# A GRU with routed experts: the order of the first loads, of the bias products and of the first x blocks

## The chip, the cores and the metric

The kernel runs on one core of one Trainium2 chip. The metric is the device time of one execution in microseconds, taken as the median of three runs. TensorE (PE in the profile), VectorE (DVE), ScalarE (ACT), GpSimd (POOL) and SyncE (SP) each run their own instruction stream in order; they meet through semaphores. SP and ACT also issue DMAs, each on a queue of its own (q1 is SP's, q10 is ACT's).

## What is computed

A GRU runs over 256 time steps for a batch of 16 rows of width 512, starting from `cond_2048`. Its states then go through eight low-rank experts, of which each row uses the two that a router picks, and the result is added to x. Cut to what matters:

```python
def cell(h, x):                     # 256 steps, each needs the one before
    gi = x @ W_ih + b_ih            # [16, 512] @ [512, 1536]
    gh = h @ W_hh + b_hh
    r = sigmoid(i_r + h_r)
    z = sigmoid(i_z + h_z)
    n = tanh(i_n + r * h_n)
    return (1 - z) * n + z * h
hs = scan(cell, cond_2048, x)       # x: [16, 256, 512]
logits = hs / norm(hs) @ router_w   # 8 experts, top 2, renormalised
out = x + sum_e combine[:, e] * (hs @ Wa[e] @ Wb[e])
```

## The kernel before

**Tiling.** The width of 512 is K = 4 slices of 128. A block of x is S = 8 time steps of 16 rows, 128 rows in all, and there are 32 blocks. Every fp32 operand is kept as two fp16 parts, a high and a low one, and a product is the sum of three part products (TERMS), so a pair of time steps takes 12 units (4 slices times 3 terms), each of four matmuls that sit side by side in the array and write the four 32-row groups of a PSUM bank. `pair_part(p, units)` does such units of pair p (steps 2p and 2p+1) of x @ W_ih into the bank `pairs[p % 2]`, on top of the biases that already stand there.

**Start.** Before step 0 can run, W_ih and W_hh (four slices each, 768 KB a slice) have to be loaded and split: ACT makes the high part of a third of a slice (`split_weights`, ACT Copy), DVE the low part, in the order of the list SPLITS: 12 entries for W_ih, then 12 for W_hh. The first three blocks of x are not transposed by DMA but by PE (`turn_first(b)`, four fp32 transposes against the identity) and then split by ACT and DVE (`split_first(b)`). The biases are spread over the rows by fp32 matmuls (`put_first_biases`: for each of the two pairs banks one matmul of 512 columns and one of 384), and `keep_biases` copies the sum to SBUF, from where ACT writes it into later banks (`put_biases`). `first_parts(k)` does the three units of slice k of pair 0. `seed(0)` and `seed_z(0)` copy the finished pair 0 from its bank into the banks `gates` and `zbank`, and `first_state_part` adds h @ W_hh: it goes through the four slices with the high weights (each waits for ACT's splits of the slice) and then through the four with the low weights (each waits for DVE's).

**Queues at the start.** ACT issues the four slices of W_ih, with x block 0 between the second and the third. SP issues three bias loads, four pieces of `cond`, the four slices of W_hh, router_w, then x block 1 once slice 1 of W_hh has landed and x block 2 once slice 2 has.

**A step.** In step n PE first does `state_part(n)` (32 matmuls of 256 columns into `gates`, 32 of 128 into `zbank`). DVE transposes the gates (the row `tr<-gates`, once a step), and DVE and ACT work through r, z, n and the new state (`st`), which PE waits for in step n+1. Behind the state part PE does what can be done meanwhile: units of the next pairs (`pair_ahead`), and expert products from step 9 on. The order on PE before step 0 and in it is: pair 0, units 0 to 5 of pair 1, `turn_first(1)`, `first_state_part`, units 6 to 11 of pair 1, `turn_first(2)`. At the end ACT does `split_first(0)` after its ninth split, `keep_biases` after its thirteenth, the seeds after its sixteenth.

Of the kernel before, what the change touches and what calls it, by code (L numbers as in the profile page):

```python
# [12 lines left out]
P = 128  # L13
# [15 lines left out]
def gru_moe_kernel(nc, x, cond, W_ih, W_hh, b_ih, b_hh, router_w, Wa, Wb, out):  # L29
# [23 lines left out]
    with ExitStack() as ctx:  # L53
# [259 lines left out]
        def _(sp):  # L313
# [64 lines left out]
            sp.wait_ge(consts_ready, 2)  # L378
            groups = "(g j c) -> j g c"
            sp.dma_start(bias_h[0:P:32, HN, :], b_hh[2 * D:3 * D].rearrange("(j c) -> j c", j=K)).then_inc(bias_loaded, 16)  # L380
            sp.dma_start(bias_h[0:P:32, RG:ZG + 1, :], b_hh[0:2 * D].rearrange(groups, g=2, j=K)).then_inc(bias_loaded, 16)
            sp.dma_start(bias_i[0:P:32, :, :], b_ih.rearrange(groups, g=3, j=K)).then_inc(bias_loaded, 16)
            for j in range(K):
                sp.dma_start(cond_sb[32 * j:32 * j + B, :], cond[:, j * P:(j + 1) * P]).then_inc(cond_loaded, 16)
            for k in range(K):
                load_hh(k)
            sp.dma_start(rw32[:, :, :], router_w.rearrange("(p k) e -> p k e", k=K)).then_inc(rw_loaded, 16)
            for b in (1, 2):
                sp.wait_ge(whh_loaded[b], 16)
                load_first(b)  # L390
# [14 lines left out]
        def _(pool):  # L405
# [96 lines left out]
            def prepare_state():  # L502
# [4 lines left out]
                pool.wait_ge(primed, 2)  # L507
# [41 lines left out]
        def _(act):  # L549
            for k in range(K):  # L550
                if k == 2:
                    act.dma_start(xin[:, 0, :], x_blocks[0]).then_inc(first_loaded[0], 16)
                act.dma_start(wih32[:, k, :, :].rearrange("p g n -> p (g n)"), W_ih[k * P:(k + 1) * P, :]
                              ).then_inc(wih_loaded[k], 16)
# [107 lines left out]
            def beside(n):  # L662
# [16 lines left out]
                if n == 0:  # L679
                    split_first(2)  # L680
# [14 lines left out]

            act.wait_ge(consts_ready, 4)
            nc.scalar.activation(table_use[:, :], ones[:, :], ACT.Sigmoid)
            for n in range(N_GRU_SPLITS):
                split_weights(n)
                if n == 8:  # L700
                    split_first(0)
                if n == N_IH_SPLITS:
                    keep_biases()
                    copy_high(-1)
                    act.wait_ge(consts_ready, N_CONST)
                if n == N_IH_SPLITS + 3:
                    seed(0)
                    seed_z(0)
            split_first(1)
# [7 lines left out]
        def _(dve):  # L717
# [117 lines left out]
            def beside(n):  # L835
# [7 lines left out]
                if n < FIRST - 1:  # L843
                    split_first(n + 1)
# [10 lines left out]
            for n in range(N_GRU_SPLITS):  # L855
                split_weights(n)
                if n == 8:
# [3 lines left out]
                if n == N_IH_SPLITS:  # L861
# [8 lines left out]
        def _(pe):  # L870
# [29 lines left out]
            def pair_part(p, units):  # L900
# [3 lines left out]
                if 0 in units:  # L904
                    if p == 1:
                        pe.wait_ge(bias_kept, 1)
# [11 lines left out]
            def put_first_biases():  # L918

                pe.wait_ge(bias_loaded, 16 * 3)  # L920
                for bank in pairs:
                    nc.tensor.matmul(bank[:, 0:4 * P], spread_rows[:, :],
                                     bias_h[:, :, :].rearrange("p g c -> p (g c)"), start=True, stop=False,
                                     skip_group_check=True)
                    mm = nc.tensor.matmul(bank[:, P:4 * P], spread_rows[:, :],
                                          bias_i[:, :, :].rearrange("p g c -> p (g c)"), start=False, stop=True,
                                          skip_group_check=True)
                mm.then_inc(bias_done, 1)
# [134 lines left out]
            def pair_ahead(n):  # L1063
# [4 lines left out]
                if p < T // 2:  # L1068
                    pair_part(p, range(UNITS[s]) if n % 2 else range(UNITS[s - 1] if n else 6, UNITS[s] if n else all_units))
# [80 lines left out]
```

## Time and profile before

| | us |
|---|---|
| median of three runs | 1009.57 |
| the three runs | 1009.29, 1009.57, 1010.45 |
| the profiled execution | 1010.27 |
| span of the profiled execution | 1008.5 |
| PE busy | 977.9 (97%) |
| DVE busy | 878.0 (87%) |
| ACT busy | 689.5 (68%) |

The span is what the profile shows, from the first instruction to the last; 1.77 us of the profiled execution lie around it. The shares say little about the change, which touches only the first 35 us or so: there PE waits for loads, and from step 0 on the steps follow one another with nothing between them.

### The profile page before, as it was taken

Reading aid. Unit: us, or ns where it says so; the run is one execution under the profiler, and the core shown is the slowest. Engines: PE = TensorE matmul, PEld = TensorE weight load, DVE = VectorE, ACT = ScalarE, POOL = GpSimd, SP = SyncE. Lnnn points to the kernel's source line nnn. Section 1 sums busy time; section 2 is a strip of 40 time slices with the busy share of each in tenths; the row PEclk is TensorE's granted clock in tenths of the full one; section 3 lists DMA queues with packets and bytes.
Section 4 is the critical chain, followed back from the end, with each engine's and each line's share of the span. In section 5 each row is a group of like instructions: output and inputs, shape, how many; then the busy total and the mean of one; then the engine's idle time right before and its main releaser. Section 6 shows DMA issues by size and latency. Waiting matters only on the chain.

```text
span 1008.5 us, 60534 instructions
## 1 busy us (share of the span) xinstructions
PE 977.9 (97%) x28939; PEld 668.9 (66%) x20799; DVE 878.0 (87%) x3637; ACT 689.5 (68%) x2696; POOL 292.9 (29%) x755
## 2 busy tenths in 40 slices
PE   4789999999999999999999999999999999999997
PEld 2456666666667666677666666666676676676674
DVE  6889888888888888888888888888888888888887
ACT  6687766776766676666677676677666667666664
POOL 1032323332323332323332332332233332233223
PEclk9999999999999999999999999999999999999999
DMA  8321111111111111111111111101111101110000
GB/s 298 93 81 31 28 33 31 27 30 32 29 31 33 28 27 35 27 31 33 29 25 35 28 32 29 33 23 35 30 30 30 32 22 35 31 30 20 14 9 29
DMA packets 49360, 38.83 MB, mean 39 GB/s; under 512 B 34532, under 2 KB 38972, under 8 KB 49084
## 3 DMA queue, kind: packets, MB, share of 16 engines
q1 hardware_dynamic: 48236, 31.41, 11.5%
q8 instruction: 198, 3.24, 1.3%
q10 hardware_dynamic: 848, 3.54, 1.0%
q14 instruction: 78, 0.64, 0.2%
HBM read 18.94 MB, written 8.39 MB: 27 GB/s over the span
## 4 chain that ended last, share of the span: by engine, by line
PE 91%; DVE 4%; DMA 2%; ACT 1%; issue 1%; SPq 0%; POOL 0%; DVEq 0%; POOLq 0%
PE pairs L882 17%; PE ybank L882 12%; PE gates L962 11%; PE gates L967 11%; PE pairs L873 8%; PE ybank L873 5%; PE zbank L882 5%; PE zbank L873 5%; PE obank L882 5%; PE nbank L882 5%; PE obank L873 3%; PE nbank L873 3%; DMA whh<-in_L_cond_W_hh 1%; DVE tr L747 1%; PE ybank L999 1%; DMA xin<-in_x 1%
## 5 line engine op out<-in xcount | busy, mean ns | idle before, releaser
L882 PE MATMUL pairs<-wx,xs 128*32 128x384 f16 x4096 | 281.4, 328 | 0.2 <-DVE wx L727 0.2
L609 ACT ACTIVATE rr<-pre 128x64 f32<-128x64 f32 x256 | 65.7, 257 | 245.8 <-DVE pre L750 245.8
L882 PE MATMUL ybank<-hparts,wa 128*128 128x128 f16 x2048 | 194.1, 219 | 0.0
L882 PEld LDWEIGHTS ybank<-hparts,wa 128*128 128x128 f16 x2048 | 159.9, 98 | 29.8 <-issue 16.7
L873 PE MATMUL ybank<-hparts,wa 128*128 128x128 f16 x1024 | 178.3, 219 | 0.0
L463 POOL TENSOR_TENSOR y<-y 128x128 f16<-128x128 f32 x256 | 106.2, 435 | 247.3 <-ACT y L660 241.8
L873 PE MATMUL pairs<-wx,xs 128*32 128x384 f16 x2048 | 174.6, 327 | 0.0
L882 PEld LDWEIGHTS pairs<-wx,xs 128*32 128x32 f16 x4096 | 108.5, 97 | 95.0 <-issue 55.3
L962 PE MATMUL gates<-whh,st 128*32 128x256 f16 x4080 | 157.3, 273 | 12.7 <-DVE st L776 12.2
L962 PEld LDWEIGHTS gates<-whh,st 128*32 128x32 f16 x4080 | 107.4, 96 | 76.8 <-ACT gates L581 47.1
L967 PE MATMUL gates<-whh,hparts 128*32 128x256 f16 x4080 | 157.1, 273 | 0.0
L873 PE MATMUL zbank<-whh,hparts 128*32 128x128 f16 x4080 | 145.4, 219 | 0.0
L882 PE MATMUL zbank<-whh,hparts 128*32 128x128 f16 x4080 | 145.4, 219 | 0.0
L747 DVE STREAM_TRANSPOSE tr<-gates 128x256 f32<-128x256 f32 x256 | 114.6, 447 | 33.7 <-PE gates L967 22.6
L882 PEld LDWEIGHTS zbank<-whh,hparts 128*32 128x32 f16 x4080 | 113.0, 97 | 15.3
L967 PEld LDWEIGHTS gates<-whh,hparts 128*32 128x32 f16 x4080 | 111.3, 97 | 1.4
L581 ACT ACTIVATE gates<-pairs,step_rows 128x256 f32<-128x256 f32 x256 | 109.9, 429 | 0.1
L617 ACT ACTIVATE zz<-pre 128x64 f32<-128x64 f32 x256 | 65.7, 257 | 50.9 <-DVE pre L760 49.2
L882 PE MATMUL obank<-wb,y 128*32 128x512 f16 (+1 forms) x980 | 97.7, 379 | 0.0
L882 PE MATMUL nbank<-wb,y 128*32 128x512 f16 x976 | 96.2, 379 | 0.0
L772 DVE SCALAR_TENSOR_TENSOR u<-nn,omz 128x64 f32<-128x64 f32 x256 | 57.5, 225 | 43.0 <-ACT nn L621 41.7
L588 ACT ACTIVATE zbank<-pairs,step_rows 128x128 f32<-128x128 f32 x256 | 84.8, 331 | 0.0
(137 smaller groups left out, 1803.1 us busy)
## 6 DMA issues: line engine op xcount, KB each, us to landing
out<-outb SPq DMA_DIRECT2D x63, 128.0 KB
xin<-in_x SPq DMA_DIRECT2D x58, 128.0 KB
wih<-in_L_cond_W_ih ACTq DMA_DIRECT2D x4, 768.0 KB, 7.8
whh<-in_L_cond_W_hh SPq DMA_DIRECT2D x4, 768.0 KB, 11.8
wih<-in_L_ffn_Wb SPq DMA_DIRECT2D x8, 256.0 KB, 2.7
xs<-xh SPq DMA_TRANSPOSE x116, 3.1
wih<-in_L_ffn_Wa SPq DMA_DIRECT2D x4, 256.0 KB, 5.2
whh<-in_L_ffn_Wa SPq DMA_DIRECT2D x4, 256.0 KB, 2.9
```

Of the source, the lines that this page charges most:

```text
L463: nc.gpsimd.tensor_tensor(y[:, m % YB, 1, :], y32[:, m % 2, :], y[:, m % YB, 0, :], ALU.subtract).then_inc(ylo_ready, 1)
L581: nc.scalar.activation(gates[:, 0:2 * P], pairs[n // 2 % 2][:, 0:2 * P], ACT.Copy, scale=step_rows[:, q:q + 1]).then_inc(seeded, 1)
L588: nc.scalar.activation(zbank[:, 0:P], pairs[n // 2 % 2][:, 2 * P:3 * P], ACT.Copy, scale=step_rows[:, q:q + 1]).then_inc(z_seeded, 1)
L609: nc.scalar.activation(rr[:, :], pre[:, RG, :, :].rearrange("p k b -> p (k b)"), ACT.Sigmoid, scale=1 / PROD_SCALE).then_inc(r_ready, 1)
L617: nc.scalar.activation(zz[:, :, :].rearrange("p k b -> p (k b)"), zpre, ACT.Sigmoid, scale=1 / PROD_SCALE).then_inc(z_ready, 1)
L747: nc.vector.transpose(tr[:, 0:2 * K, :].rearrange("p (g k) c -> p g k c", k=K), gates[:, 0:2 * P].rearrange("p (g c k) -> p g k c", g=2, k ...
L772: nc.vector.scalar_tensor_tensor(out=u[:, :], in0=nn[:, :], scalar=PART_SCALE, in1=omz[:, :], op0=ALU.mult, op1=ALU.mult).then_inc(u_ready, 1)
L873: return nc.tensor.add_instruction(mybir.InstMatmult(name=nc.get_next_instruction_name(), engine=mybir.EngineType.PE, start_tensor_calc=start,
L882: return nc.tensor.matmul(out, lhsT, rhs, start=start, stop=stop, skip_group_check=True)
L962: nc.tensor.matmul(gates[32 * j:32 * j + 32, 0:2 * P], st[:, k, :], whh[:, 1, k, j, 0:2 * P], start=False, stop=False, skip_group_check=True)
L967: mm = nc.tensor.matmul(gates[32 * j:32 * j + 32, 0:2 * P], prior[:, k, :], whh[:, 0, k, j, 0:2 * P], start=False, stop=(k == K - 1), skip ...
L999: mm = nc.tensor.matmul(bank[:, P:P + (2 - part) * NE], hf[:, part, k, :], rw[:, 0:2 - part, k, :], start=(part == 0 and k == 0), stop=(pa ...
```

## The change

The SP queue now begins with x block 0, then slices 0 and 1 of W_ih, then `cond`. Each further slice is asked for when an earlier one has landed: slices 2 and 3 of W_ih after slice 0, slice 0 of W_hh after slice 1 of W_ih, slice 1 after slice 2, slices 2 and 3 after slice 3. router_w and the x blocks 1 and 2 come behind these. ACT's queue now has only the three bias loads.

The bias matmuls are done for bank 0 alone; ACT copies the whole bank into bank 1, which PE has cleared with four more matmuls by zero. All of pair 0 waits for these copies (`bias_kept` of 2), which stand on ACT between the eleventh and the twelfth split. Pair 1 is done whole ahead of the first state part, x block 1 is transposed at the end of step 0 and x block 2 at the end of step 1. The seeds stand two splits later on ACT, and the split of x block 0 six earlier.

```diff
@@ SP @@
-            sp.wait_ge(consts_ready, 2)
-            groups = "(g j c) -> j g c"
-            sp.dma_start(bias_h[0:P:32, HN, :], b_hh[2 * D:3 * D].rearrange("(j c) -> j c", j=K)).then_inc(bias_loaded, 16)
-            sp.dma_start(bias_h[0:P:32, RG:ZG + 1, :], b_hh[0:2 * D].rearrange(groups, g=2, j=K)).then_inc(bias_loaded, 16)
-            sp.dma_start(bias_i[0:P:32, :, :], b_ih.rearrange(groups, g=3, j=K)).then_inc(bias_loaded, 16)
-            for j in range(K):
-                sp.dma_start(cond_sb[32 * j:32 * j + B, :], cond[:, j * P:(j + 1) * P]).then_inc(cond_loaded, 16)
+            load_first(0)
+            load_ih(0)
+            load_ih(1)
+            load_cond()
+            sp.wait_ge(wih_loaded[0], 16)
+            load_ih(2)
+            load_ih(3)
             for k in range(K):
+                if k + 1 < K:
+                    sp.wait_ge(wih_loaded[k + 1], 16)
                 load_hh(k)
+            sp.wait_ge(whh_loaded[0], 16)
             sp.dma_start(rw32[:, :, :], router_w.rearrange("(p k) e -> p k e", k=K)).then_inc(rw_loaded, 16)
             for b in (1, 2):
-                sp.wait_ge(whh_loaded[b], 16)
                 load_first(b)
@@ ACT @@
-                nc.scalar.activation(bias_sums[:, :], pairs[1][:, P:4 * P], ACT.Copy).then_inc(bias_kept, 1)
+                nc.scalar.activation(bias_sums[:, :], pairs[0][:, P:4 * P], ACT.Copy).then_inc(bias_kept, 1)
+                nc.scalar.activation(pairs[1][:, :], pairs[0][:, :], ACT.Copy).then_inc(bias_kept, 1)
...
-                if n == 0:
-                    split_first(2)
+                if n + 1 < FIRST:
+                    split_first(n + 1)
...
+            load_biases()
...
-                if n == 8:
+                if n == 2:
                     split_first(0)
-                if n == N_IH_SPLITS:
+                if n == N_IH_SPLITS - 2:
                     keep_biases()
+                if n == N_IH_SPLITS + 2:
                     copy_high(-1)
                     act.wait_ge(consts_ready, N_CONST)
-                if n == N_IH_SPLITS + 3:
+                if n == N_IH_SPLITS + 5:
                     seed(0)
                     seed_z(0)
-            split_first(1)
@@ PE @@
-                    if p == 1:
-                        pe.wait_ge(bias_kept, 1)
+                    if p < 2:
+                        pe.wait_ge(bias_kept, 2)
...
+                if n == 1:
+                    turn_first(2)
...
                 if n == 0:
-                    turn_first(2)
+                    turn_first(1)
...
-            for g, n_cols in ((gates, 2), (zbank, 1)):
+            for g, n_cols in ((gates, 2), (zbank, 1), (pairs[1], 4)):
...
-            pair_part(1, range(6))
-            turn_first(1)
+            pair_part(1, range(K * len(TERMS)))
             first_state_part()
```

DVE's low splits of the x blocks move with ACT's (block 0 after the third split, blocks 1 and 2 in steps 1 and 2).

This is the head of SP's instructions before, with the semaphores that each row waits for (`whh` from `in_L_cond_W_hh` is a slice of W_hh, `wih` from `in_L_cond_W_ih` one of W_ih, `xin` a block of x):

```order
L380 DMA bias_h<-in_L_cond_b_hh 4x128 [waits consts_ready]
L381 DMA bias_h<-in_L_cond_b_hh 4x2x128
L382 DMA bias_i<-in_L_cond_b_ih 4x3x128
L384 DMA cond_sb<-in_cond 16x128 x4
L335 DMA whh<-in_L_cond_W_hh 128x1536 x4
L387 DMA rw<-in_L_ffn_router_w 128x32
L315 DMA xin<-in_x 128x1x512 [waits whh1_loaded]
L315 DMA xin<-in_x 128x1x512 [waits whh2_loaded]
```

And this is the same place in the changed kernel:

```order
L315 DMA xin<-in_x 128x1x512
L379 DMA wih<-in_L_cond_W_ih 128x1536 x2
L385 DMA cond_sb<-in_cond 16x128 [waits consts_ready]
L385 DMA cond_sb<-in_cond 16x128 x3
L379 DMA wih<-in_L_cond_W_ih 128x1536 [waits wih0_loaded]
L379 DMA wih<-in_L_cond_W_ih 128x1536
L335 DMA whh<-in_L_cond_W_hh 128x1536 [waits wih1_loaded]
L335 DMA whh<-in_L_cond_W_hh 128x1536 [waits wih2_loaded]
L335 DMA whh<-in_L_cond_W_hh 128x1536 [waits wih3_loaded]
L335 DMA whh<-in_L_cond_W_hh 128x1536
L399 DMA rw<-in_L_ffn_router_w 128x32 [waits whh0_loaded]
L315 DMA xin<-in_x 128x1x512 x2
```

W_ih moved from ACT's queue to SP's, ahead of W_hh, and the x blocks 1 and 2 lost their own waits but stand behind all of W_hh.

On PE, around the first state part, stood before (pair 1's first half, the transposes of x block 1, the first rows of the state part):

```order
L882 MATMUL pairs<-wx,xs 32x384 [waits xlo_ready,bias_kept]
L882 MATMUL pairs<-wx,xs 32x384 x3
L873 MATMUL pairs<-wx,xs 32x384 x4
L882 MATMUL pairs<-wx,xs 32x384 x8
L873 MATMUL pairs<-wx,xs 32x384 x4
L882 MATMUL pairs<-wx,xs 32x384 x4
L890 MATMUL ybank<-ident,xin 128x128 [waits first1_loaded]
L890 MATMUL ybank<-ident,xin 128x128 x3
L950 MATMUL gates<-whh,hparts 32x256 [waits both_parts_ready,hi_split,z_seeded,seeded]
```

In the changed kernel the last rows of the state part are followed on PE by:

```order
L962 MATMUL gates<-whh,st 32x256 [waits weights_split]
L962 MATMUL gates<-whh,st 32x256 x3
L962 MATMUL zbank<-whh,st 32x128 x4
L906 MATMUL ybank<-ident,xin 128x128 [waits first1_loaded]
L906 MATMUL ybank<-ident,xin 128x128 x3
L974 MATMUL gates<-whh,st 32x256 [waits hhi_ready,seeded]
```

The transposes of x block 1, with their wait for its load, moved from ahead of the first state part to ahead of step 1's.

On ACT the part between the eleventh split and the seeds reads now:

```order
L572 ACTIVATE wx<-wih 128x4x128 [waits wih3_loaded] x2
L607 ACTIVATE bias_sums<-pairs 128x384 [waits bias_done]
L608 ACTIVATE pairs<-pairs 128x512
L572 ACTIVATE wx<-wih 128x4x128 [waits wih3_loaded]
L572 ACTIVATE whh<-whh 128x4x128 [waits whh0_loaded] x3
L619 ACTIVATE hparts<-st 128x4x16 [waits hhi_ready]
L572 ACTIVATE whh<-whh 128x4x128 [waits whh1_loaded,consts_ready]
L572 ACTIVATE whh<-whh 128x4x128 [waits whh1_loaded] x2
L595 ACTIVATE gates<-pairs,step_rows 128x256 [waits pair_done]
```

Before, the bias copy stood after the thirteenth split and was one instruction, not two.

## Rows read from the trace of the kernel before

**Rows 1.** The page: its first line.

```profile
span 1008.5 us, 60534 instructions
```

**Rows 2.** The chain of waits in order of time: start us, us, what.

```profile
17.37 5.92 DMA xin<-in_x
23.33 1.11 PE ybank L890 x4
...
30.78 0.46 DVE tr L747
...
34.42 0.46 DVE tr L747
```

**Rows 3.** The timeline, PE and SP, 3 to 32 us: start us, us, what.

```profile
3.26 0.53 SPq L382 DMA_DIRECT2D bias_i<-in_L_cond_b_ih  x1
...
11.01 0.50 PEld L922 LDWEIGHTS pairs<-bias_h,spread_rows 128*128 128x128 f32 x2 [0.37 <-DMA bias_i<-in_L_cond_b_ih]
...
14.16 1.73 PE L922 MATMUL pairs<-bias_h,spread_rows 128*128 128x512 f32 x2
...
16.47 0.35 PE L882 MATMUL pairs<-wx,xs 128*32 128x384 f16 x4
...
24.38 0.40 PE L950 MATMUL gates<-whh,hparts 128*32 128x256 f16 x4
...
26.59 0.43 PE L950 MATMUL gates<-whh,st 128*32 128x256 f16 x4
...
31.00 0.33 PE L882 MATMUL pairs<-wx,xs 128*32 128x384 f16 x4
31.16 0.33 PE L873 MATMUL pairs<-wx,xs 128*32 128x384 f16 x4
```

**Rows 4.** The timeline of ACT, 15 to 25 us.

```profile
15.67 1.67 ACT L558 ACTIVATE wx<-wih 128x512 f16<-128x512 f32 x3 [1.62 <-DMA wih<-in_L_cond_W_ih]
...
17.77 0.47 ACT L593 ACTIVATE bias_sums<-pairs 128x384 f32<-128x384 f32 x1
...
19.84 0.42 ACT L581 ACTIVATE gates<-pairs,step_rows 128x256 f32<-128x256 f32 x1
...
20.45 4.26 ACT L558 ACTIVATE whh<-whh 128x512 f16<-128x512 f32 x8
24.60 0.59 ACT L562 ACTIVATE xs<-ybank 128x512 f16<-128x512 f32 x1
```

**Rows 5.** The timeline of DVE, 21 to 30 us.

```profile
21.10 4.90 DVE L727 SCALAR_TENSOR_TENSOR whh<-whh 128x512 f16<-128x512 f32 x8 [0.27 <-ACT whh L558]
...
27.07 0.45 DVE L747 STREAM_TRANSPOSE tr<-gates 128x256 f32<-128x256 f32 x1 [0.84 <-PE gates L950]
```

**Rows 6.** Windows: busy us (instructions) of each engine, granted PE clock, DMA share, GB/s.

```profile
0.00:2.00 2.00, 0.00 (x0) 0.00 (x0) 0.00 (x0) 0.00 (x0) 1.47 (x10) 1.00 0.18 28
...
6.00:10.00 4.00, 0.04 (x1) 0.07 (x2) 3.44 (x6) 2.78 (x6) 0.00 (x0) 1.00 1.04 268
10.00:18.00 8.00, 8.00 (x48) 3.65 (x36) 4.83 (x9) 4.48 (x9) 0.63 (x2) 1.00 1.01 409
...
20.00:22.40 2.40, 0.00 (x0) 0.00 (x0) 2.13 (x5) 2.40 (x6) 0.00 (x0) 1.00 0.69 206
22.40:29.20 6.80, 5.87 (x93) 3.55 (x86) 5.72 (x16) 3.94 (x11) 0.00 (x0) 0.50 0.59 133
...
30.00:50.00 20.00, 13.98 (x516) 9.69 (x366) 17.54 (x75) 13.00 (x46) 0.00 (x0) 1.00 0.34 96
```

**Rows 7.** Loads by line: time from issue to landing, W_ih first, then W_hh.

```profile
L553 ACTq DMA_DIRECT2D wih<-in_L_cond_W_ih x4: 330/421/782, 0.7 to 3.2; - x4
...
DMA to landing us min/median/max: 4.3/7.8/12.4
```

**Rows 8.** The same of W_hh.

```profile
L335 SPq DMA_DIRECT2D whh<-in_L_cond_W_hh x4: 423/432/460, 5.8 to 7.2; - x4
...
DMA to landing us min/median/max: 9.7/11.8/13.9
```

More of the change, by code:

```diff
@@ L376, in beside, with load_ih, load_cond @@
                     store(i - 2, s - 5)
[L378 to L384 removed]
+            def load_ih(k):
+                sp.dma_start(wih32[:, k, :, :].rearrange("p g n -> p (g n)"), W_ih[k * P:(k + 1) * P, :]
+                             ).then_inc(wih_loaded[k], 16)
+            def load_cond():
+                sp.wait_ge(consts_ready, 1)
+                for j in range(K):
+                    sp.dma_start(cond_sb[32 * j:32 * j + B, :], cond[:, j * P:(j + 1) * P]).then_inc(cond_loaded, 16)
+            load_first(0)
[5 more added lines that the diff above has]
+            load_ih(3)
             for k in range(K):
+                if k + 1 < K:
+                    sp.wait_ge(wih_loaded[k + 1], 16)
                 load_hh(k)
+            sp.wait_ge(whh_loaded[0], 16)
             sp.dma_start(rw32[:, :, :], router_w.rearrange("(p k) e -> p k e", k=K)).then_inc(rw_loaded, 16)
             for b in (1, 2):
[L389 removed]
                 load_first(b)
@@ L549, in _, with load_biases @@
         def _(act):
[L550 to L554, printed above, removed]
+            groups = "(g j c) -> j g c"
+            def load_biases():
+                act.wait_ge(consts_ready, 2)
+                act.dma_start(bias_h[0:P:32, HN, :], b_hh[2 * D:3 * D].rearrange("(j c) -> j c", j=K)).then_inc(bias_loaded, 16)
+                act.dma_start(bias_h[0:P:32, RG:ZG + 1, :], b_hh[0:2 * D].rearrange(groups, g=2, j=K)).then_inc(bias_loaded, 16)
+                act.dma_start(bias_i[0:P:32, :, :], b_ih.rearrange(groups, g=3, j=K)).then_inc(bias_loaded, 16)
             def split_weights(n):
@@ L842, in beside @@
                     rank_experts(i - 1)
-                if n < FIRST - 1:
-                    split_first(n + 1)
+                if 1 <= n < FIRST:
+                    split_first(n)
                 if 0 <= n - 1 < len(SPLITS) - N_GRU_SPLITS:
@@ L856, in _ @@
                 split_weights(n)
-                if n == 8:
+                if n == 2:
                     split_first(0)
@@ L920, in put_first_biases @@
                 pe.wait_ge(bias_loaded, 16 * 3)
[L921 to L928, printed above, removed]
+                nc.tensor.matmul(pairs[0][:, 0:4 * P], spread_rows[:, :], bias_h[:, :, :].rearrange("p g c -> p (g c)"),
+                                 start=True, stop=False, skip_group_check=True)
+                nc.tensor.matmul(pairs[0][:, P:4 * P], spread_rows[:, :], bias_i[:, :, :].rearrange("p g c -> p (g c)"),
+                                 start=False, stop=True, skip_group_check=True).then_inc(bias_done, 1)
             def first_parts(k):
@@ L1067, in pair_ahead @@
                     pair_part(p - 1, range(UNITS[s - 1], all_units))
-                if p < T // 2:
-                    pair_part(p, range(UNITS[s]) if n % 2 else range(UNITS[s - 1] if n else 6, UNITS[s] if n else all_units))
+                if n and p < T // 2:
+                    pair_part(p, range(UNITS[s]) if n % 2 else range(UNITS[s - 1], UNITS[s]))
             def wide_step(n):
```

4 lines of the change are left out of this document (2 added, 2 removed).

## The prediction

> **What bounds the kernel now.** I read the chain of waits first, because the change lies in the start and only the chain says what ends last there. It runs over the load of x block 1, asked for at 17.37 and landed at 23.33, to PE's transposes of that block [rows 2], and only behind these does the first state part begin, at 24.38 [rows 3]. Its end releases DVE's transpose of the gates at 27.07 [rows 5]. I call that moment T0. From there the steps follow one another: the transposes of steps 1 and 2 begin at 30.78 and 34.42 [rows 2], 3.71 and 3.64 us apart. Nothing in the change touches a step after the second, so the rest of the span [rows 1] moves by as much as the start does. The question is what T0 becomes and whether steps 0 and 1 keep their length.
>
> Three things come close together ahead of T0. PE: 24.38 plus the eight groups of the state part. ACT: its eight last splits of W_hh run without a gap from 20.45 to 24.60 [rows 4], 0.52 us each. DVE: its eight last splits run from 21.10 to 26.00 [rows 5], 0.61 us each, and the last group of the state part, at 26.59 [rows 3], needs them. So taking the wait for x block 1 out of PE's way gains little by itself: DVE's splits would still hold T0 near 26.00 + 0.48 (26.59 to 27.07) = 26.5. Only loads of W_ih that come earlier let ACT and DVE begin earlier.
>
> The second view is the clock. The granted clock is 1.00 from 20.0 to 22.4, while PE does nothing, and 0.50 (1.2 GHz) from 22.4 to 29.2, though PE is busy for 5.87 of those 6.80 us; then it is back at 2.4 GHz [rows 6]. A group of the state part has 256 + 128 columns, as many as a unit of a pair. In the slow stretch seven groups take from 24.38 to 26.59, 0.316 us each; in the fast one a unit takes 0.16 (31.00 to 31.16) [rows 3].
>
> **The loads.** The slices of W_ih take 4.3 to 12.4 us from issue to landing; the last, issued at 3.2, lands at 15.6 [rows 7], and ACT's tenth split starts on it at 15.67 after 1.62 us of waiting [rows 4]. The slices of W_hh take 9.7 to 13.9 us and are issued from 5.8 to 7.2, so the first lands at 15.5, the last at 21.1 [rows 8]. The first slice of W_hh thus lands together with the last of W_ih. At 409 GB/s [rows 6] a slice (0.786 MB) takes 1.92 us. With W_ih ahead in one queue, its last slice has one slice less before it: 15.6 - 1.9 = 13.7. The stretch from 6 to 10 us moved 268 GB/s instead of 409 [rows 6], 4 x (1 - 268/409) = 1.4 us lost; if that goes too, it is 12.3. I take 13.0, because part of that stretch was small pieces (biases, router_w) which partly remain. The last slice of W_hh has the same bytes ahead of it: 19.7 to 21.1, and I take 20.5. The waits on SP keep two slices asked for at a time; what is queued behind them is router_w and x blocks 1 and 2. These land some 2.2 us after W_hh, as before (21.1 to 23.33): about 22.7. PE has to have transposed block 1 when step 1's state part begins, some 1.1 us ahead of its end, so only a landing after 26.2 (24.7 + 3.64 - 1.1 - 1.05, worked out below) would hold a step back, by as much as it is later. I put it at nothing.
>
> **ACT and DVE.** From 13.0 ACT does two splits (1.1) to 14.1. The bias copies come next. They need the bias matmuls: the last bias load was issued at 3.26 and PE began on it at 11.01 [rows 3]; issued on ACT's queue at about the same time, it comes at about the same time. One bank took 11.01 to 14.16 [rows 3], so the copies can start at 14.2. They are 0.47 [rows 4] plus a copy of 512 columns, like ACT's split of an x block at 0.59 [rows 4]: to 15.2. The remaining 13 splits are 13 x 0.53 = 6.9, the copy of the state 0.15, the seeds 0.6 (19.84 to 20.45) [rows 4]: to 22.9. From the landing of the last slice at 20.5 alone it would be 22.1, so ACT's own work decides. DVE takes 0.61 against ACT's 0.53, so over the last six splits after the seeds it falls 0.5 behind, and ends 1.2 us after ACT: 24.1. Then 0.1 to PE, and the 0.48 from PE's last group to the transpose: T0 = 24.7, a gain of 2.4. Bounds: if the biases come soon (6 us instead of 11) and W_ih at 12.3, ACT ends 0.7 earlier, a gain of 3.1; if W_ih comes at 13.7 and the last slice at 21.1 it is 0.6 later, a gain of 1.8; with a pause between the slices, since each is asked for only when another has landed, I allow 0.7 more, a gain of 1.1.
>
> **PE ahead of T0.** Removed: one bank of bias matmuls, 16.47 - 14.16 = 2.3 us [rows 3]; added: four matmuls by zero at 4.5, where PE is idle. All of pair 0 now waits for the bias copies, 15.2. The work behind it is 24 units, 24 x 0.16 = 3.9 fast or 7.7 slow. The seeds need pair 0 by 19.1 or so: slow it is there at 15.2 + 3.8 = 19.0. So it hides under ACT's splits either way, and pair 1's second half, 1.9 us at the slow clock, leaves step 0, where it was hidden too.
>
> **Steps 0 and 1.** The length of a step is its chain over DVE and ACT. Step 0 has lost its units and DVE its split of an x block just ahead of 30.78: 3.64 instead of 3.71, 0.1 gained. Step 1 gets the transposes of x block 2, 1.05 us at the slow clock (23.33 to 24.38) [rows 2, 3]. At 2.4 GHz the PE of step 1 has eight groups (1.3), five units (0.8) and these (0.6 to 1.05): about 3 of 3.64 us, hidden. But between the end of pair 1 and step 1 PE has little: the state part in pieces as splits arrive, four transposes, and some 1.5 us of nothing. That is the kind of stretch after which the clock fell at 22.4. If it falls, step 1 runs at 1.2 GHz: a group is 0.316 us, two thirds of it gates: 8 x 0.21 = 1.7, then 0.84 for z, 5 x 0.32 = 1.6, 1.05: 5.2 us against 3.64, 1.55 lost. If the clock rises early in step 1 only the gates are late, 0.9; if it stays down through step 2 (1.7 + 0.84 + 7 x 0.32 = 4.8), 1.1 more, 2.7 in all. I take 1.6 with a little for the state part. The steps afterwards have PE busy 13.98 of 20 us and the clock at 1.00 [rows 6].
>
> **The forecast: earlier start, clock down in step 1.** 2.4 + 0.1 - 1.6 = 0.9 gained, less about 0.1 that I leave for the seeds: 0.8. The profiled execution would be 1010.27 - 0.8 = 1009.5; it was 0.70 above the median, so the median becomes 1009.57 - 0.8 = 1008.8.
>
> **The rivals.**
> (A) The clock stays up. For it: PE works nearly without a pause from 11 to 20 us and has pieces until T0, and the later steps keep the clock with 70% [rows 6]. Against it: from 21 to step 1 PE has about 2.5 us of work in 6. Gain 2.4 + 0.1 = 2.5: 1007.1.
> (B) The array is slow through the pairs as well. The first bias bank took 3.15 us and the second 2.31 [rows 3], under a granted clock of 1.00 throughout; so the array seems to have been at 1.2 GHz in the first and the record not to show it. If PE stays slow until T0: 15.2 + 7.7 = 22.9, then seven groups of 0.316 and 0.48 more: T0 = 25.6, a gain of 1.5; with 0.1, 1.6 and 0.1 as in the forecast nothing is left of it: 1009.7.
> The Trainium skill (TensorE: Matmul & The Clock Gate, "The HAM clock gate") says that the slow state is the default and that activity releases it. The row of 3.15 against 2.31 agrees. By that rule pair 0 begins fast only if the bias matmuls have released the clock, as they had by 16.47 before; it is the case for B.
> (C) The loads become slower, and the kernel too. One queue with two slices asked for replaces two queues with all asked for. If the rate stayed at the 268 GB/s of the stretch from 6 to 10, x block 0 and eight slices (6.55 MB) would take 24.4 us, after 2 us in which hardly anything moves [rows 6]: the last slice lands at 26.3. From there to T0 it is one split of ACT, three of DVE and 0.6, 3.0 in all: T0 = 29.3, 2.2 later, and the clock adds up to 1.6: 1011.8 to 1013.4. With the clock's 1.6, slower than before begins where the last slice lands at 22.6, a mean of 318 GB/s from 2 us on. Against it: 409 GB/s over 8 us [rows 6], and before, these 6.55 MB took from 2 to 21.1, a mean of 343 with other loads among them.
> (D) The change doesn't do what it says: the last slice of W_ih lands at 15.6 as now, since x block 0 stands ahead and a pause may follow slice 1. Then ACT's work from there (two splits, the copies, 13 splits, 0.75) ends at 25.4, and T0 is 27.2: no gain, and the clock's 1.6 on top: 1011.1.
>
> **How the numbers follow.** Forecast 0.44, A 0.27, B 0.17, C 0.05, D 0.07. A measurement tells 0.2%, 2.0 us, from no change: under 1007.55 is faster, over 1011.6 slower. A lies over the bound in four cases of five and the forecast's early end adds a little: faster 0.24. Slower is C and the part of D in which the clock stays down through step 2: 0.07. The rest, 0.69, is within. The range leaves out C and D (0.12) and the earliest end of A (T0 0.7 earlier, 1006.4; some 0.04): it goes from 1006.9, a little below A, to 1010.5, which holds B and a forecast with 1.1 more for a slow step 2 (1009.9).
>
> **What would show it.** In the changed profile: the tenth split on ACT at about 13 and not 15.7; ACT without gaps from 14 to 23; T0 at 24.7; x block 1 landed before it; a granted clock of 0.50 somewhere between 22 and 33 and a distance of over 4.5 us between the transposes of steps 1 and 2, against 3.64. The prediction is wrong if T0 is above 26 (the loads), if the clock never falls (A), or if a step after the second changes its length.

## The result, and the profile after

The changed kernel is slightly slower: 1010.9 us against 1009.57 us (medians of 22 runs each), a ratio of 1.0012 with a 95% interval of 1.0006 to 1.0017. That is less than the 0.2% that the prediction called a difference, but it lies on the other side of no change than the forecast of 1008.8, and outside the range of 1006.9 to 1010.5. The profiled execution took 1011.0 us with a span of 1009.1. Of the runs below, one of the ten of b_loads, at 1032.05 us, is a slow one, with a lower clock on record; without it the median of b_loads is 1011.38 instead of 1011.44.

The start of a step is best read from DVE's transpose of its gates. These rows are the timeline of DVE in the changed kernel (start us, us, what), the first four steps:

```profile
25.70 0.45 DVE L763 STREAM_TRANSPOSE tr<-gates 128x256 f32<-128x256 f32 x1 [0.17 <-PE gates L962]
...
30.19 0.45 DVE L763 STREAM_TRANSPOSE tr<-gates 128x256 f32<-128x256 f32 x1 [1.47 <-PE gates L979]
...
34.68 0.45 DVE L763 STREAM_TRANSPOSE tr<-gates 128x256 f32<-128x256 f32 x1 [0.78 <-PE gates L979]
...
38.79 0.44 DVE L763 STREAM_TRANSPOSE tr<-gates 128x256 f32<-128x256 f32 x1
```

T0 is 25.70 instead of 27.07 [rows 5], 1.37 us earlier. But steps 0 and 1 are 4.49 us long, where they were 3.71 and 3.64 [rows 2, 5], and step 2 is 4.11. From step 3 on the two kernels run alike in these two traces. The tenth transpose stands at 60.66 in this trace and at 59.97 in that of before, and from there to the end of the span it is 948.4 and 948.5 us. So the whole difference is made in the first three steps and before.

What waits where ahead of T0 shows in the chain of waits of the changed kernel (start us, us, what):

```profile
1.59 6.15 DMA wih<-in_L_cond_W_ih
8.14 5.77 DMA wih<-in_L_cond_W_ih
14.30 8.42 DMA whh<-in_L_cond_W_hh
22.74 0.64 ACT whh L572
23.40 1.91 DVE whh L743 x3
25.70 0.46 DVE tr L763
```

The load of x block 1, which was in the chain before [rows 2], is gone. In its place stands the last slice of W_hh: asked for at 14.30, landed at 22.7. Before, it landed at 21.1 [rows 8].

The clock and the loads of the changed kernel, windows with the columns of [rows 6]:

```profile
2.00:6.00 4.00, 0.93 (x7) 0.67 (x7) 0.00 (x0) 1.49 (x2) 1.91 (x20) 1.00 0.79 202
6.00:10.00 4.00, 1.09 (x4) 0.72 (x4) 1.58 (x3) 2.19 (x5) 0.00 (x0) 1.00 0.92 329
10.00:18.00 8.00, 4.99 (x32) 2.02 (x24) 7.55 (x14) 7.36 (x15) 1.16 (x2) 0.90 1.00 399
...
23.30:26.70 3.40, 1.78 (x44) 1.15 (x44) 3.09 (x9) 1.36 (x4) 0.00 (x0) 1.00 0.75 178
26.90:33.40 6.50, 5.15 (x88) 3.21 (x64) 4.32 (x21) 4.18 (x16) 0.00 (x0) 0.50 0.33 98
34.00:50.00 16.00, 10.87 (x412) 7.69 (x296) 13.54 (x56) 10.54 (x36) 0.00 (x0) 1.00 0.28 79
```

The granted clock is 0.50 (1.2 GHz) from 26.9 to 33.4, that is nearly all of step 1's work on PE, after a stretch in which PE was busy 1.78 of 3.40 us. Step 1's state part at the slow clock reads as follows (timeline of PE):

```profile
25.64 0.66 PE L906 MATMUL ybank<-ident,xin 128*128 128x128 f32 x4
28.25 1.04 PE L974 MATMUL gates<-whh,st 128*32 128x256 f16 x16 [1.95 <-DVE st L792]
29.05 1.09 PE L979 MATMUL gates<-whh,hparts 128*32 128x256 f16 x16
```

PE stands idle for 1.95 us until the new state is there, and then takes from 28.25 to 30.14 for the gates.

One more thing is needed to read the totals. The profiled execution of before was 0.7 us above its median. Profiled once more, the kernel before had T0 at 26.40 in an execution of 1009.75 us (before_again below), where the median on that chip is 1009.77. I take this as the nearer to its usual start; two traces can't show more.

### The profile page after: what moved, and what is told of

The parts are those of the page before. It is cut to its first block, busy times and chain, and to the rows that moved or that the text cites. A ratio compares the mean times of both kernels' runs of the same rounds, so it can differ in the third digit from the quotient of the medians.

```text
span 1009.1 us, 60536 instructions
## 1 busy us (share of the span) xinstructions
PE 977.7 (97%) x28939; PEld 668.4 (66%) x20799; DVE 878.2 (87%) x3637; ACT 690.6 (68%) x2697; POOL 293.4 (29%) x755
## 4 chain that ended last, share of the span: by engine, by line
PE 91%; DVE 5%; DMA 2%; ACT 1%; issue 0%; SPq 0%; DVEq 0%
PE pairs L898 17%; PE ybank L898 12%; PE gates L974 11%; PE gates L979 11%; PE pairs L889 8%; PE ybank L889 5%; PE zbank L898 5%; PE zbank L889 5%; PE obank L898 5%; PE nbank L898 5%; PE obank L889 3%; PE nbank L889 3%; DMA wih<-in_L_cond_W_ih 1%; DMA whh<-in_L_cond_W_hh 1%; DVE tr L763 1%; PE ybank L1011 1%
## 5 line engine op out<-in xcount | busy, mean ns | idle before, releaser
L898 PEld LDWEIGHTS ybank<-hparts,wa 128*128 128x128 f16 x2048 | 159.9, 98 | 29.9 <-issue 16.7
```

The lines of the kernel that those rows point to most:

```text
L898: return nc.tensor.matmul(out, lhsT, rhs, start=start, stop=stop, skip_group_check=True)
```

## The experiments

All distances are read from DVE's transposes of the gates, as above. T9 is the tenth of them; the span beyond it was 948.2 to 948.8 us in every kernel, so T9 carries the time. Each row of the table but the medians is one execution. The last column is the median of the kernel before on the chip where that kernel ran.

| kernel | T0 | steps 0, 1, 2, 3, 4 | T9 | median us | before, same chip |
|---|---|---|---|---|---|
| before | 27.07 | 3.71, 3.64, 3.66, 3.64, 3.65 | 59.97 | 1009.57 | |
| before_again | 26.40 | 3.65, 3.65, 3.64, 3.65, 3.65 | 59.23 | one run, 1009.75 | 1009.77 |
| changed | 25.70 | 4.49, 4.49, 4.11, 3.64, 3.64 | 60.66 | 1010.90 | 1009.57 |
| after_again | 25.41 | 4.49, 3.87, 4.11, 3.89, 4.20 | 60.55 | one run, 1010.79 | 1009.42 |
| a_fill | 25.61 | 3.65, 3.65, 4.11, 3.77, 4.31 | 59.69 | 1009.50 | 1009.73 |
| a_split3 | 25.99 | 4.49, 4.17, 3.65, 3.91, 3.64 | 60.45 | 1010.51 | 1009.73 |
| a_askall | 25.19 | 4.49, 4.68, 4.11, 3.64, 3.65 | 60.35 | 1010.22 | 1009.73 |
| b_turns | 26.22 | 4.15, 3.65, 4.11, 3.64, 3.64 | 60.00 | 1010.67 | 1009.73 |
| b_loads | 28.39 | 3.65, 3.65, 3.65, 3.65, 3.65 | 61.23 | 1011.44 | 1009.77 |
| a_best1 | 25.40 | 3.64, 3.65, 3.65, 3.91, 3.65 | 58.49 | 1008.55 | 1009.77 |
| a_best2 | 24.81 | 3.65, 3.65, 3.64, 3.91, 3.65 | 57.89 | 1008.41 | 1009.77 |
| a_nofill2 | 24.49 | 4.49, 3.87, 3.65, 3.91, 3.63 | 58.63 | 1009.23 | 1009.42 |
| a_real | 25.01 | 3.65, 3.65, 3.64, 3.91, 3.63 | 58.08 | 1008.38 | 1009.42 |

**Is it the clock, or the work that now stands in the steps? (a_fill)** Thirteen matmuls whose results nobody reads fill PE's two idle places.

```diff
+            def filler(n):
+                for _ in range(n):
+                    nc.tensor.matmul(ybanks[1][:, :], whh[:, 0, 0, 0, 0:P],
+                                     whh[:, 0, 0, :, :].rearrange("p j c -> p (j c)")[:, 0:4 * P],
+                                     start=True, stop=True, skip_group_check=True)
@@ first_state_part, behind the third group of high weights @@
+                        if pw == 0 and k == K - 2:
+                            filler(6)
@@ grouped_step @@
                 if n == 0:
                     turn_first(1)
+                    filler(7)
```

> The changed kernel with thirteen added fp16 matmuls of 512 columns on PE, whose results nobody reads: six behind the third group of the first state part, seven behind the transposes of x block 1 in step 0. My theory: the clock fell at 26.8 because PE had little to do from 22.6 to 28.2, and the slow clock alone makes steps 0 and 1 4.49 us long. Then the granted clock stays at 1.00 from 20 us on, the transposes of the gates of steps 0, 1 and 2 are 3.65 apart again, and the time is 1.7 us below the changed kernel's, about 1009.2. Rival: the steps are long because the transposes of the x blocks stand in them and the state part waits behind; then they stay near 4.49 whatever the clock, and the time is the changed kernel's 1010.9 or, with the added matmuls in the way, more.

Steps 0 and 1 went back to 3.65 us each, with the x blocks still transposed in them, and the clock stayed up: it is the clock. The windows of a_fill:

```profile
22.60:26.70 4.10, 3.82 (x62) 2.02 (x55) 3.81 (x11) 1.92 (x4) 0.00 (x0) 1.00 0.85 166
26.90:33.40 6.50, 5.32 (x164) 3.65 (x122) 5.11 (x24) 5.13 (x18) 0.00 (x0) 1.00 0.42 123
...
36.90:40.10 3.20, 1.09 (x38) 0.70 (x29) 2.89 (x14) 2.12 (x8) 0.00 (x0) 1.00 0.20 59
40.50:43.60 3.10, 3.10 (x68) 1.59 (x33) 2.37 (x12) 1.61 (x7) 0.00 (x0) 0.50 0.31 90
```

The expectation was right on the steps. Of the time it expected 1.7 us and 1.4 came. That is 0.23 us under the kernel before, which is no difference by that comparison's interval (0.9989 to 1.0007). The last two rows say where some of it went: the clock fell once more, from 40.3 to 43.8, after a stretch in which PE was busy 1.09 of 3.20 us. In the changed kernel the same stretch had 1.99 us of work and no fall:

```profile
36.90:40.10 3.20, 1.99 (x76) 1.49 (x56) 3.13 (x12) 1.74 (x6) 0.00 (x0) 1.00 0.32 98
```

Steps 3 and 4 cost 0.78 us there. Step 3 of this program is the lightest for PE (three units behind the state part); when it comes 1.8 us earlier, its idle time falls into this stretch. The changed kernel isn't free of this fall either: its second execution had it, at 41.0 (after_again).

**Step 2: two splits on DVE (a_split3).**

```diff
-                if 1 <= n < FIRST:
-                    split_first(n)
+                if n in (1, 3):
+                    split_first(1 + n // 3)
```

> The changed kernel with DVE's split of x block 2 in step 3 instead of step 2, where a split of Wa stands too. My theory: in step 2 the two together (37.62 to 38.79) hold DVE's transpose of the gates of step 3 by 0.45 us; then the distance from the transpose of step 2 to that of step 3 falls from 4.11 to 3.66, and nothing comes back in step 4 beyond 0.2, since DVE has no transpose of gi_n in step 3. Time 1010.5. Rival: the Wa split alone or late arrival of its data holds DVE, and the distance stays above 4, or the delay only moves to step 4.

In the changed kernel DVE has this in step 2, ahead of step 3's transpose:

```profile
37.62 0.65 DVE L737 SCALAR_TENSOR_TENSOR xs<-obank,xs 128x512 f16<-128x512 f32 x1
...
38.20 0.67 DVE L743 SCALAR_TENSOR_TENSOR wa<-wih,wa 128x512 f16<-128x512 f32 x1
38.79 0.44 DVE L763 STREAM_TRANSPOSE tr<-gates 128x256 f32<-128x256 f32 x1
```

With the split in step 3, step 2 is 3.65 us and step 3 is 3.91. So 0.46 is gone and 0.26 comes back, a little more than the 0.2 expected: DVE has no transpose of gi_n in step 3, but it has a split of Wa in every step from 2 on. The median, 1010.51, says the same within its noise. The rival (the split of Wa alone) falls, since in the kernel before that split stands in step 2 by itself and costs nothing.

**The loads: the waits (a_askall).** SP's waits for landed slices are taken out, the order stays.

```diff
-            sp.wait_ge(wih_loaded[0], 16)
...
-                if k + 1 < K:
-                    sp.wait_ge(wih_loaded[k + 1], 16)
...
-            sp.wait_ge(whh_loaded[0], 16)
```

> The changed kernel with all loads of SP asked for at once in the same order, without the waits for landed slices. My theory: the pause between slices costs part of the late landing of W_hh (DMA share 0.65 from 8 to 9 us, slice 2 of W_ih issued only at 7.75), about 0.7 us; the last slice lands at 22.0 instead of 22.7 and the gates of step 0 are transposed at 25.0 instead of 25.7. Rival: the number of bytes ahead and the late start of the first slice decide; then W_hh lands at 22.7 as in the changed kernel. A third: with everything asked for at once the transfers share the engines, the slices of W_ih land later (after 14.5) and T0 rises above 25.7.

The last slice of W_hh, asked for at 7.4, landed 14.4 us later at 21.8, T0 was 25.19. The landing is 0.2 us earlier than expected and T0 0.2 later, so by this pair of traces the waits cost 0.9 us of landing and 0.5 of T0. Half of the bytes that the changed kernel is behind at 18 us are lost between 6 and 10 us, the rest in the stretches beside it:

```profile
2.00:6.00 4.00, 1.03 (x8) 0.80 (x9) 0.00 (x0) 1.49 (x2) 1.92 (x20) 1.00 0.80 228
6.00:10.00 4.00, 0.99 (x4) 0.58 (x4) 1.60 (x3) 2.23 (x5) 0.00 (x0) 1.00 1.03 392
10.00:18.00 8.00, 5.14 (x36) 2.03 (x28) 7.67 (x14) 7.47 (x16) 1.16 (x2) 0.90 1.01 416
```

That is 392 GB/s against 329 from 6 to 10 us (against 285 to 340 in the five executions with the waits), and 416 against 399 from 10 to 18. From 2 to 6 us it moves 228 where the changed kernel moves 202; seven executions with x block 0 at the head move 199 to 231 there, with the waits or without, so this is not the waits. The kernel before moves 360 or 361.

T0 itself spreads. Four executions with the changed kernel's loads and order on PE, ACT and DVE before T0 (changed, after_again, a_fill, a_split3) have it at 25.41 to 25.99, with the last slice landed at 22.45 to 23.04; the two with all asked for in the same order (a_askall, a_best1) have it at 25.19 and 25.40. There the slice landed at 21.8 and 22.2. By the means the waits cost 0.7 us of landing and 0.4 of T0. The third theory, that W_ih would be held up, falls: ACT's tenth split began at 13.78 instead of 13.94.

**One part of the change alone (b_turns, b_loads).** b_turns is the kernel before with the two x blocks transposed at the end of steps 0 and 1 (the moved `turn_first` calls on PE, with the splits of ACT and DVE). b_loads is the kernel before with the new loads on both queues, and bias products, PE, ACT and DVE as before.

```diff
@@ b_turns, PE @@
             pair_part(1, range(6))
-            turn_first(1)
             first_state_part()
@@ b_loads, SP @@
+            load_first(0)
+            load_ih(0)
+            load_ih(1)
+            load_cond()
+            sp.wait_ge(wih_loaded[0], 16)
...
```

> The kernel before with one part of the change alone: x block 1 transposed at the end of step 0 and block 2 at the end of step 1, with their splits. My theory from the prediction: PE no longer waits for x block 1, and DVE's splits hold the gates of step 0 at 26.5 instead of 27.07, 0.5 us gained; steps 0 and 1 are 3.65 if the clock is up and longer by up to 0.85 each if it has fallen; step 2 loses 0.45 to the two DVE splits, as in the changed kernel. Rival: the part alone gives most of the changed kernel's earlier start (25.7), and the loads give nothing.

> The kernel before with the new loads alone (order, waits, biases on ACT's queue); bias matmuls for both banks and the order on PE, ACT and DVE as before. My theory: the last slice of W_hh lands at 22.7 as in the changed kernel, x block 1 behind it at 24.5, and PE stands on that: 1.05 of transposes, then the state part of 1.3 to 2.5, so T0 is at 27.3 to 28.5, 0.2 to 1.5 later than before; time 1010.5. Rival: the earlier W_ih brings T0 forward even so, to 26 or less.

b_turns has T0 at 26.22. That is 0.3 earlier than expected, but only 0.2 earlier than the second execution of before: PE's wait for x block 1 was worth next to nothing, since DVE's splits hold T0 there. Its step 0 is 4.15 us under a slow clock (0.50 from 22.6 to 29.4), 0.5 lost, step 2 is 4.11 as expected, and its time of 1010.67 is 0.9 above before, interval 1.0001 to 1.0019.

b_loads is slower by 1.7 us (1.0008 to 1.0027). x block 1, now behind all of W_hh, lands at 24.7 instead of 23.3 and PE stands before it; behind it the first state part runs with the granted clock at 0.50 (21.3 to 28.1). The chain of waits of b_loads:

```profile
16.48 8.23 DMA xin<-in_x
...
24.75 1.12 PE ybank L905 x4
25.86 0.34 PE gates L965 x4
...
28.39 0.46 DVE tr L762
```

The range expected for T0 held, the time was 0.9 above what I expected. Each of these two parts alone makes the kernel slower. The third part, the new order of the bias products and of pair 1, was not run alone, and neither were the loads and the moved transposes together without it; so what it adds to the 25.7 isn't shown.

**How the start spreads (before_again, after_again).** Both kernels unchanged, profiled once more.

> The kernel before, unchanged, to see how its start spreads. Its profiled execution was 0.7 us above the median of its runs. My theory: T0 (27.07 then) varies with the landing of x block 1 and the place where the clock falls, so a second execution near the median has T0 at 26.4 or a step 0 of 3.65 with the same rest, 948.5 us from the tenth transpose to the end. Rival: the starts agree within 0.2 and the spread is in the rest.

> The changed kernel once more, to see how its start spreads. My theory: T0 25.4 to 26.0, the clock falls within 0.5 us of 26.8 and steps 0 and 1 are 4.2 to 4.5 us long, step 2 4.1; the tenth transpose at 60.2 to 61.0. Rival: the clock falls at another place, as it did in the second execution of the kernel before (25.0 instead of 22.4), and the lengths of steps 0 and 1 change by up to 0.8 each.

The kernel before had T0 at 26.40 and a step 0 of 3.65, with 948.8 us behind T9: the spread is in the start. The load of x block 1 landed at the same time, 23.35 against 23.33, so half of that theory falls: the 0.67 us of T0 come from the clock alone. It fell at 24.9 instead of 22.4, when half of the state part was done. The transposes of x block 1 and the first group of the state part in before_again (timeline of PE):

```profile
23.35 0.66 PE L890 MATMUL ybank<-ident,xin 128*128 128x128 f32 x4 [3.55 <-DMA xin<-in_x]
23.94 0.29 PE L950 MATMUL gates<-whh,hparts 128*32 128x256 f16 x4
```

Before, the same transposes took 1.11 us [rows 2]. The windows of before_again:

```profile
22.40:24.80 2.40, 1.43 (x36) 1.03 (x40) 2.40 (x5) 2.40 (x6) 0.00 (x0) 1.00 1.05 193
25.10:28.10 3.00, 3.00 (x56) 1.19 (x40) 2.65 (x11) 0.73 (x4) 0.00 (x0) 0.50 0.45 129
```

The two executions differ by 0.74 us at T9. Against this second one the changed kernel is 1.43 us later, which agrees with the 1.33 between the medians; against the first one it was 0.69. The changed kernel's second execution had the clock low from 27.4 to 30.9 and once more from 41.0 to 44.5. Steps 0 to 4 lost 2.3 us to these and to DVE together (their lengths less 3.65 each); in the first execution it was 2.1, in other places. Both theories held in part: the lengths of the steps moved by up to 0.6 and the sum hardly.

**All losses taken out (a_best1, a_best2, a_nofill2, a_real).** a_best1 joins a_fill, a_split3 and a_askall and adds this at the end of step 3:

```diff
                 if n == 1:
                     turn_first(2)
+                if n == 3:
+                    filler(5)
```

a_best2 also asks for x block 0 behind slice 1 of W_ih:

```diff
-            load_first(0)
             load_ih(0)
             load_ih(1)
+            load_first(0)
@@ ACT and DVE @@
-                if n == 2:
+                if n == 5:
                     split_first(0)
```

a_nofill2 is a_best2 without the eighteen added matmuls. a_real is a_nofill2 with the units of pair 1 in the idle places, which is work that has to be done anyway:

```diff
-            pair_part(1, range(K * len(TERMS)))
+            pair_part(1, range(4))
@@ first_state_part @@
+                        if pw == 0 and k == K - 2:
+                            pair_part(1, range(4, 8))
@@ grouped_step @@
                     turn_first(1)
+                    pair_part(1, range(8, 12))
```

> The changed kernel with all loads of SP asked for at once, DVE's split of x block 2 in step 3, the thirteen added matmuls of before and five more at the end of step 3, where the clock fell at 40.1 without them. My theory: the three losses add up. T0 at 25.2, the clock at 1.00 from 20 us to step 12, the distances between the transposes of the gates all 3.65 except up to 0.25 more in one of steps 3 and 4 (two DVE splits); the tenth transpose at 58.2, the time 1008.4, 2.5 under the changed kernel and 1.2 under the kernel before. Rival: the added matmuls of step 3 stand ahead of the state part of step 4 and cost what they save, or the clock falls somewhere later; then the time stays near 1009.5.

> The same with x block 0 asked for behind slice 1 of W_ih instead of ahead of slice 0, and its splits after the sixth entry instead of the third. My theory: x block 0 at the head costs the loads some 0.5 to 1.3 us (202 to 228 GB/s from 2 to 6 us with it at the head, 360 without): the first split of ACT starts at 6.0 instead of 7.7, the last slice of W_hh lands at 21.2 instead of 21.8, and T0 is 24.6, 0.6 under the kernel that differs in this alone; time 1007.8. Rival: ACT's and DVE's own work behind the bias copies sets T0, since it runs without a gap from 13.8; then T0 stays at 25.1.

> The kernel with the loads asked for at once, x block 0 behind slice 1 and DVE's split of x block 2 in step 3, but without the eighteen added matmuls. My theory: T0 stays at 24.8, the clock falls between 26 and 27.5 and steps 0 and 1 are 4.2 to 4.5 us long, so most of the 2.1 us that the better loads give against the kernel before are lost again: time 1009.9, 1.5 above the kernel with the added matmuls. Rival: the better loads carry the gain and the added matmuls only a few tenths: 1008.7.

> The same with the twelve units of pair 1 spread over the idle places instead of added matmuls: four ahead of the first state part, four behind its third group, four at the end of step 0. My theory: that is 0.65 us of work in each place where the added matmuls had 1.3 and 1.5; PE is then busy some 2.4 of 3.4 us around the gap and under half of step 0, which is near what stood ahead of the fall at 26.8, so the clock may still fall, but later than without it: steps 0 and 1 lose 0 to 1.3 us together, time 1008.5 to 1009.7. Rival: the units in step 0 hold step 1's state part or seed 1, and step 0 is longer than 3.65 with the clock up.

a_best1 and a_best2 came to 1008.55 and 1008.41, ratios to before of 0.9988 (0.9979 to 0.9997) and 0.9989 (0.9980 to 0.9998). The losses add up: steps 0 to 2 are 3.65, the clock is up from 20 us on in both. The x block behind slice 1 brings T0 0.6 earlier as expected in this pair; the three executions with it there (a_best2, a_nofill2, a_real) have T0 at 24.49 to 25.01, by the means 0.5 earlier than the two with it at the head. These rows of a_best2 answer to those of a_askall above:

```profile
2.00:6.00 4.00, 0.93 (x7) 0.66 (x7) 0.00 (x0) 1.61 (x3) 1.92 (x20) 1.00 0.91 365
6.00:10.00 4.00, 0.74 (x4) 0.77 (x5) 3.57 (x6) 2.99 (x6) 0.00 (x0) 1.00 0.80 251
```

What 2 to 6 us gain, 6 to 10 lose: 365 and 251 GB/s here, 228 and 392 in a_askall, the same bytes by 10 us. So the last slice of W_hh still landed at 21.8, not at 21.2 (21.5 in a_nofill2, 22.1 in a_real): what came earlier is W_ih (ACT's first split at 5.78 instead of 8.08), and with it everything ACT and DVE had to do. In the medians the 0.6 is 0.14, less than these comparisons can tell.

a_nofill2 lost less than I expected. T0 was 24.49, steps 0 and 1 were 4.49 and 3.87, since the clock rose again at 29.9, and its median is 0.8 above a_best2, not 1.5; each against the kernel before on its own chip, it is 1.2 (0.2 and 1.4 below). Its ratio to before is 1.0000 (0.9991 to 1.0009). a_real has the clock at 1.00 on record from the start past step 12 and steps 0 to 2 of 3.65, at 1008.38 us, 1.0 below before (0.9981 to 0.9999) and 2.5 below the changed kernel's median. Its windows:

```profile
22.60:26.70 4.10, 2.54 (x60) 1.38 (x56) 3.74 (x12) 1.84 (x7) 0.00 (x0) 1.00 0.60 156
26.90:33.40 6.50, 5.10 (x176) 3.76 (x132) 5.28 (x24) 4.78 (x16) 0.00 (x0) 1.00 0.37 110
```

Between 22.6 and 26.7 it has 2.54 us of work where the changed kernel had 1.92:

```profile
22.60:26.70 4.10, 1.92 (x52) 1.15 (x44) 3.72 (x11) 1.92 (x4) 0.00 (x0) 1.00 0.82 185
```

That is one execution. Where the clock falls differs between executions of the same kernel. The medians on one chip, 1008.38 for a_real and 1009.23 for a_nofill2, say that the spread units help in most runs; that the clock always stays up is not shown.

## Why the prediction was wrong

- **What bounds the start.** Right. With PE's wait for x block 1 taken out alone, T0 was to be 26.5 because DVE's splits hold it; b_turns had 26.22, and before_again 26.40 even with the wait in place.
- **The loads: the step that failed first.** "I take 20.5" for the last slice of W_hh, with 21.1 as the late bound, on the ground that "the same bytes" stand ahead of it. It landed at 22.7. ACT's tenth split came at 13.94 instead of 13.0. The waits on SP leave a pause, worth 0.9 us of landing by a_askall and 0.7 by the means of six executions. I had allowed 0.7 of T0 for a pause in the bounds but put nothing on it in the sum. T0 moved by 1.37 instead of 2.4: inside the bounds of 1.1 to 3.1, and 1.0 us off the value taken.
- **The loads without the waits.** Another 1.3 us separate the forecast of 20.5 from the 21.8 of a_askall. I had taken the slow stretch of the kernel before (268 GB/s from 6 to 10 us) as a loss that would go, and it only moved: with x block 0 at the head 2 to 6 us is the slow one (202 GB/s in the changed kernel, 228 in a_askall, against 360 before), and with the block behind slice 1 it is 6 to 10 again (251 in a_best2). With all asked for at once the last slice landed at 21.1 to 22.2 in whatever order, never near 20.5; why not earlier stays open. x block 0 at the head is not what held that slice, but it made W_ih late, and cost 0.5 of T0 where the waits were gone; what it cost the changed kernel itself, with the waits, was not run.
- **ACT and DVE.** The amounts of work were right and began late: the bias copies were to start at 14.2 and started at 14.99, the seeds were to come at about 19.1 and came at 20.06, as the tenth split was 0.94 late. "ACT's own work decides" was wrong with the late slice: ACT waited 0.40 us for it until 22.74. From there to T0 it was 2.96 us, near the 3.0 that rival C has for this.
- **The bias products.** Right: they took from 10.16 to 13.4 and the copies stood ready for them. The wait of pair 0 for the copies left PE idle from 13.4 to 16.2 (the trace names a split of DVE as what ended it, but by the kernel's waits pair 0 needs the copies, done at 15.96, and only the first three splits), after which the clock fell at 16.5 and rose at 19.9. That is rival B's case in part, and it hid under ACT's splits: the seeds began as soon as ACT was free, 20.06. In a_askall, where ACT was free earlier, they waited 0.21 us for pair 0.
- **Steps 0 and 1: right in mechanism, and in size partly by luck.** 1.6 us was taken for the clock in step 1 and 0.1 gained in step 0. The two steps together lost 1.63, and a_fill gives them back with the clock alone. Against steps of 3.65 the five executions in which the clock fell between 26.3 and 27.4 lost 1.06 to 1.87 in these two steps, and this one 1.68. And it is half in each: the transpose that ends the distance of step 0 waits for step 1's slow state part, and step 1's distance is set by PE's slow work up to step 2's (30.19 to 34.68, with the state part fast again).
- **Step 2: a term that was missing.** "Nothing in the change touches a step after the second" is false. In after_again even steps 3 and 4 lost 0.8 us to a second fall of the clock, which neither trace of the kernel before shows. In every trace of the changed kernel step 2 is 4.11: DVE's split of x block 2 follows its transposes by one step, into step 2, where the splits of Wa begin. I followed the moved transposes on PE and not all of what they issue on DVE; the price is 0.45 us.
- **The base: a term that was missing.** The profiled execution of before was 0.70 us above the median. I carried the difference over as if it were the same for both kernels. It was not: 0.74 of it lies in the start of this one execution (T0 at 27.07 against 26.40, step 0 at 3.71 against 3.65), the very stretch that the change rebuilds: the clock had fallen 2.4 us earlier in it, ahead of the whole state part. What the new start was to save was partly not there in the usual execution.

The account: forecast 0.8 gained. T0 takes 1.0 of it, step 2 0.45, and the steps 0 and 1 0.13, against 0.1 left for the seeds; that makes -0.7, as the two traces show. The base takes 0.7 more: -1.4 against a measured -1.33. The base rests on the one trace of before_again. The rival that came nearest in its number is D (1011.1), but not in its mechanism: W_ih did land earlier. In mechanism it is C, given 0.05: with the clock's 1.6 on top it puts the edge of "slower than before" at a last slice landed at 22.6, and the slice landed at 22.7. C's own times of 1011.8 and above were not reached. Of the three signs that the prediction named as wrong, T0 above 26 and a clock that never falls did not come; a changed step behind the second did.

## What to carry to other kernels

Work taken off an engine's path leaves it idle, and on TensorE an idle stretch can cost more later than it saved (here 1.63 us in two steps against 1.37 of an earlier start): move work that has to be done anyway into the gap ahead of a critical chain, rather than doing it early. When a transfer or a transpose is moved, follow each instruction it feeds on every engine to the step in which it lands, and see what stands there already. And where a change rebuilds a stretch of a few microseconds, one trace of before is not enough as a base: profile that stretch twice.

## What the runs showed of the hardware

- The granted clock reads 1.00 from the start in all traces, but PE's first instructions are slow: four fp32 transposes take 1.09 us at 6.11 and 0.66 us at 25.64 in the changed kernel, both under a granted clock of 1.00, and 1.12 us at 24.75 in b_loads under 0.50. By these durations PE began at 1.2 GHz and rose without a rise in the record; the first level that the record shows isn't to be trusted. This also answers the 3.15 against 2.31 us of the bias products [rows 3].
- A clock that had fallen stayed down for 3.4 to 6.8 us in the traces here, with PE busy for most of it. What that costs depends on what lies under it: 1.6 us on steps 0 and 1 of the changed kernel (1.1 in its second execution), 0.8 on steps 3 and 4 of a_fill, and in the kernel before, where one execution had the state part and step 0 under it and the other only half of the state part, 0.7 between the two.
- A block of x (128 rows of 2 KB) at the head of the queue, with the slices of 6 KB rows behind it, gave 199 to 231 GB/s from 2 to 6 us in seven executions; the slices at the head gave 355 to 368 in six. From 6 to 10 us it is the other way round where all was asked for at once (392 and 394 against 251 to 290). The cause was not looked into further; the first slice was also asked for 0.87 us later, at 1.59.
- Two slices asked for at a time, each further one when an earlier had landed, gave 285 to 340 GB/s from 6 to 10 us, against 392 and 394 with the same order and all asked for at once.
